# Graph attention on one core: the last pair of edge blocks in three pieces, and matmuls with one-hot matrices in place of a closing scatter

## What is computed

```python
h   = relu(layernorm(x)) @ W_node.T                 # per node, 4 heads x 32
att = leaky(sum([h[src], h[dst], edge @ W_edge.T] * a))   # per edge and head, slope 0.2
m   = max(segment_max(att, dst), 0)
ex  = exp(att - m[dst])
den = segment_sum(ex, dst) + (E - deg) * exp(-m)
out = x + segment_sum(ex / den[dst] * h[src], dst)
```

## Time and profile before

| | us |
|---|---|
| median of 3 runs | 4960.86 |
| the 3 runs | 4958.59, 4969.13, 4960.86 |
| profiled execution, its own time | 4962.95 |
| its span, first to last instruction | 4955.9 |
| DVE busy | 2412.0 (49%) |
| ACT busy | 1368.3 (28%) |
| PE busy | 777.3 (16%) |
| POOL busy | 3712.2 (75%) |

### The profile page before, as it was taken

The page is one execution under the profiler, slowest core; times in us unless marked ns, Lnnn a source line. Parts: engine busy times, 40 slices in busy tenths (PEclk is TensorE's granted clock), DMA queues, the critical chain, the costliest instruction groups (busy, mean ns, idle before and its releaser), DMA issues.

```text
span 4955.9 us, 14358 instructions
## 1 busy us (share of the span) xinstructions
PE 777.3 (16%) x1453; PEld 390.6 (8%) x1453; DVE 2412.0 (49%) x2384; ACT 1368.3 (28%) x1021; POOL 3712.2 (75%) x3530
## 2 busy tenths in 40 slices
PE   5321111111111111111111111111111111111100
PEld 3310000000000000000000000000000000000000
DVE  7337454545445454454544545445454454544543
ACT  7013232222322222222222322223222232222320
POOL 6667777777777777777777777777777777777766
PEclk9555555555555555555555555555555555555555
DMA  7234444343443434434344343433434434343353
GB/s 250 90 132 119 140 123 128 114 137 114 126 125 114 137 114 128 123 115 137 114 127 123 114 136 114 129 121 115 137 114 128 122 115 136 114 131 120 116 170 104
DMA packets 171831, 627.97 MB, mean 127 GB/s; under 512 B 72897, under 2 KB 73666, under 8 KB 155426
## 3 DMA queue, kind: packets, MB, share of 16 engines
q0 software_dynamic: 115936, 252.37, 21.0%
q1 hardware_dynamic: 55874, 375.39, 20.1%
HBM read 382.66 MB, written 244.86 MB: 127 GB/s over the span
## 4 chain that ended last, share of the span: by engine, by line
POOL 70%; issue 24%; another core or an unknown queue 2%; ACT 2%; DVE 1%; PE 0%; DMA 0%; POOLq 0%; ACTq 0%; DVEq 0%; SPq 0%
POOL slots L308 69%; ACT pen L375 1%; DVE pen L482 0%; PE ae L792 0%; DVE slots L496 0%; ACT big L392 0%; ACT slots L391 0%; POOL tdst_scratch L311 0%; ACT R L421 0%; PE wexp L785 0%; DMA state_scratch<-R 0%; DVE V L636 0%; DVE slots L501 0%; DMA cols<-in_cols_dram 0%
## 5 line engine op out<-in xcount | busy, mean ns | idle before, releaser
L308 POOL DMA_INDIRECT slots<-rows_scratch,idx x3224 | 3421.5, 1061 | 1066.5 <-issue 1066.5
L803 PE MATMUL ae<-eab,w_att 128*128 128x416 f32 x992 | 650.6, 829 | 3796.2 <-DMA eab<-in_ea_dram 2539.1
L603 DVE TENSOR_TENSOR z<-slots,big 128x104 f32<-128x104 f32 (+1 forms) x125 | 43.1, 345 | 2116.3 <-DMA slots<-rows_scratch,idx 1887.3
L636 DVE TENSOR_TENSOR_SCAN V<-A,V 128x1848 f32<-128x1848 f32 x248 | 993.7, 4007 | 35.4 <-issue 4.8
L421 ACT COPY R<-V 128x1716 f32<-128x1716 f32 x248 | 777.8, 3136 | 339.1 <-DVE V L636 196.7
L417 ACT ACTIVATE A<-D 128x1848 f32<-128x1848 f32 x246 | 419.7, 1706 | 744.7 <-DVE V L636 410.3
L803 PEld LDWEIGHTS ae<-eab,w_att 128*128 128x128 f32 x992 | 296.0, 313 | 4150.4 <-issue 3384.4
L626 DVE TENSOR_TENSOR V<-slots,wexp 128x1716 f32<-128x1716 f32 x125 | 404.8, 3239 | 22.4 <-issue 21.0
L626 DVE TENSOR_TENSOR V<-slots,extra 128x1716 f32<-128x1716 f32 x123 | 398.2, 3237 | 22.0 <-issue 16.3
L438 ACT ACTIVATE wexp<-D 128x104 f32<-128x104 f32 x62 | 16.2, 261 | 1092.5 <-DVEq L621 628.8
L438 ACT ACTIVATE extra<-D 128x104 f32<-128x104 f32 x61 | 15.9, 261 | 1063.2 <-DVEq L621 631.2
(11 more groups left out here) (168 smaller groups left out, 602.3 us busy)
## 6 DMA issues: line engine op xcount, KB each, us to landing
state_scratch<-R SPq DMA_DIRECT2D x123, 1768.0 KB
eab<-in_ea_dram SPq DMA_DIRECT2D x126, 832.0 KB
slots<-rows_scratch,idx POOLq DMA_INDIRECT x3224
rows_scratch<-slots SPq DMA_DIRECT2D x14, 476.0 KB
tdst_scratch<-eab SPq DMA_DIRECT2D x4, 1612.0 KB
big<-tdst_scratch SPq DMA_DIRECT2D x8, 806.0 KB
big<-in_x_t_dram SPq DMA_DIRECT2D x14, 448.0 KB, 4.3
big<-in_x_dram SPq DMA_DIRECT2D x7, 896.0 KB
```

Of the source, the lines that this page charges most:

```text
L308: pool.indirect_dma_start(buf, None, table, bass.IndirectOffsetOnAxis(ap=index, axis=0)).then_inc(done, 16)
L636: nc.vector.tensor_tensor_scan(V[:, v, :], a_all, V[:, v, :], 0.0, ALU.mult, ALU.add).then_inc(scanned, 1)
L803: last = mm(ps_ae[k][:, 0:KB * Q], w_att[:, a * P:(a + 1) * P], eab[:, k, a * KB * Q:(a + 1) * KB * Q], start=a == 0, stop=a == 3)
```

## The change

The last pair is worked on in three pieces of 13, 9 and 4 columns, with three waits, copies and stores in place of two. The buffers of the end (`pen_end`, `att_end`, `D2_end`, `M`) get a place per piece, and the tail's work area moves from V[:, 0] to V[:, 1].

The scatter at the end goes, with `x_first`, its gather, `fix_i` and the spare rows of the output. In its place the fix chain computes for each partition the difference between the merged result and the one that the ordinary path gives (`att_fix`), by three more vector instructions. For each group of 7, DVE compares a row of node numbers with the place of the node to be fixed (`one_hot`, 128 x 896), PE multiplies the seven one-hot matrices with `att_fix` (seven 128 x 128 matmuls into `ps_ae`), and DVE adds the product to `xr` in two instructions (`add_fix`), ahead of the group's ordinary work. `one_hot(0)`, `one_hot(1)` and `add_fix(0)` stand ahead of the group loop; in the loop, one_hot(g + 2) and add_fix(g + 1) follow the addition of group g. The wait for x_again moves from L757 into `add_fix`.

```diff
+LAST = ((0, KB), (KB, 9), (KB + 9, KB - 9))
...
-                    for v in range(2):
-                        dve.wait_ge(gather_end[v], 16 * KB)
-                        logits(p, k, 1 - v, v, KB, att_end, att_end, pen_end[:, v:v + 1, :, :], D2_end[:, v, :])
-                        dve.wait_ge(w_ready, p + 1 + v)
-                        if v == 0:
-                            dve.wait_ge(copied, p)
-                        sums(k, v, hk(w_exp[1 - v][:, 0:H * KB]), 2 * p + 1 + v, False)
+                    for e, (o, n) in enumerate(LAST):
+                        u = (p + e) % 2
+                        c = LAST[e + 1][1] + 1 if e + 1 < len(LAST) else COL
+                        dve.wait_ge(gather_end[e], 16 * n)
+                        logits(p, k, u, M_END[e], o, n, att_end[:, e, :], hk(att_end[:, e + 1, 0:H * c]), pen_end[:, e, 0:H * (n + 1)], D2_end[:, e, 0:H * (n + 1)])
+                        dve.wait_ge(w_ready, p + 1 + e)
+                        if e != 1:
+                            dve.wait_ge(copied, p + e // 2)
+                        m = LAST[e - 1][1] if e else KB
+                        sums(k, o, n, e % 2, hk(w_exp[u][:, 0:H * n]), 2 * p + 1 + e, vcols(1 - e % 2, m + 1)[:, :, m:m + 1])
...
-            pool.wait_ge(fix_ready, 1)
-            pool.wait_ge(stored, 16 * STEPS)
-            scatter(out[:, :], fix_i[:, 0:1], x_first[:, :], fix_dma)
...
+            nc.vector.tensor_scalar(fx[:, 3 * H:4 * H], s_first[:, VAL:ROW], -1.0, None, ALU.mult)
...
-            nc.vector.tensor_tensor(hv(x_first[:, :]), hv(x_first[:, :]), hv(cf[:, 0:VAL])[:, :, 0:HD], ALU.add).then_inc(fix_ready, 1)
-
+            nc.vector.tensor_tensor(hv(f["tmp"])[:, :, 0:HD], hv(s_first[:, 0:VAL])[:, :, 0:HD], wide(f["den"][:, H:2 * H], HD), ALU.mult)
+            nc.vector.tensor_tensor(hv(cf[:, 0:VAL])[:, :, 0:HD], hv(cf[:, 0:VAL])[:, :, 0:HD], wide(f["den"][:, 0:H], HD), ALU.mult)
+            dve.drain()
+            nc.vector.tensor_tensor(hv(att_fix[:, :]), hv(cf[:, 0:VAL])[:, :, 0:HD], hv(f["tmp"])[:, :, 0:HD], ALU.subtract).then_inc(fix_ready, 1)
+
+            def one_hot(g):
+                after(dve, moved, g - 1)
+                nc.vector.tensor_tensor(hot[g % 2], firsts[:, :].rearrange("p (a j) -> p a j", a=1).broadcast_to([P, NG, P]),
+                                        fix_at[:, g * NG:(g + 1) * NG].rearrange("p (w a) -> p w a", a=1).broadcast_to([P, NG, P]),
+                                        ALU.is_equal).then_inc(hot_done, 1)
+
+            def add_fix(g):
+                if g % 2 == 0:
+                    dve.wait_ge(x_again[g // 2], 16)
+                dve.wait_ge(moved, g + 1)
+                for k, (a, b) in enumerate(((0, 4), (4, NG))):
+                    xg = xr[:, g * NG + a:g * NG + b, :]
+                    last = nc.vector.tensor_tensor(xg, xg, ps_ae[k][:, 0:(b - a) * P].rearrange("p (w d) -> p w d", d=D), ALU.add)
+                last.then_inc(moved_taken, 1)
+
+            one_hot(0)
+            one_hot(1)
+            add_fix(0)
...
-                if g % 2 == 0:
-                    dve.wait_ge(x_again[g // 2], 16)
                 dve.drain()
                 xg = xr[:, g * NG:(g + 1) * NG, :]
                 nc.vector.tensor_tensor(xg, xg, A[:, g % 2 * 1024:g % 2 * 1024 + NG * D].rearrange("p (w d) -> p w d", d=D), ALU.add).then_inc(group_done, 1)
+                if g + 2 < STEPS:
+                    one_hot(g + 2)
+                if g + 1 < STEPS:
+                    add_fix(g + 1)
...
+            pe.wait_ge(fix_ready, 1)
+            for g in range(STEPS):
+                pe.wait_ge(hot_done, g + 1)
+                after(pe, moved_taken, g)
+                for n in range(NG):
+                    last = mm(ps_ae[n // 4][:, n % 4 * P:(n % 4 + 1) * P], hot[g % 2][:, n, :], att_fix[:, :], start=True, stop=True)
+                last.then_inc(moved, 1)
```

## The result

| | before | after |
|---|---|---|
| median of the runs, us | 4967.6 (4958.6 to 4969.1) | 5008.0 (4997.8 to 5011.4) |
| ratio | 1 | 1.0077, 95% interval 1.0066 to 1.0087 |
| profiled execution: own time / span, us | 4962.95 / 4955.9 | 5011.35 / 5009.5 |
| time around the span, us | 7.05 | 1.85 |

The change makes the kernel 0.8% slower, 40 us by the medians. The two profiled executions lie 48.4 us apart (5011.35 - 4962.95), where I had forecast 29.0. The direction and the place were right, but two steps of the sum were far off and their errors had opposite signs.

The account below looks back on a forecast made before the run. POOL's gathers bound the kernel now, VectorE's paced groups after the change. Group 0 at 4848.5, 13 x 9.7, last group 7.1, then 2.9: end 4984.9 against 4955.9, +29.0; forecast 4990 us, bounds 4945 to 5008.

Parts of the forecast that it names:

- The paced state: Closing stage: VectorE gets through one instruction, drains counted, per 0.78 us; main case, slower, spanning 4970 to 5008, chance 0.66.
- the rivals without a pace: Closing stage: VectorE needs 5.5 us per group and POOL bounds, -15.8, 4945 us, chance 0.18; POOL stretched builds on that.
- The price of an instruction: VectorE's group loop: 7.00 us over nine instructions, drains counted, gives 0.78 us for each.
- The head: Last pair in three pieces: last scan ends 2.0 us earlier, s_first starts at 4807.9, last gather ends 6.2 us earlier.
- The fix chain's three instructions: Three vector instructions added between the last scan and group 0, at 0.78 us each: 2.3 us.
- Between the fix chain and group 0: one_hot(0) 1.10, seven matmuls 3.0, two additions 1.1, hand-overs 0.3: 5.5 us, so group 0 starts at 4848.5.
- The groups: Closing group loop: 12.5 instructions instead of 9, period 9.7 us instead of 7.00, 13 periods, then 7.1 for the last group.
- POOL stretched: Closing stage: VectorE's new instructions slow 98 gathers by 0.15 us each, 14.7 on the no-pace end: 4960, chance 0.06.
- The end: Behind L760: closing scatter and its wait go, POOL's drain hidden, tail shrinks from 13.0 to 2.9 us, -10.1.
- Around the span: Execution's own time outside the span: 7.05 us, carried over from the kernel before.
- The signs I gave: Trace after: L747 over 9 us apart, idle at drains, last gather about 50 us before last L760, s_first near 4808.

Follow-up runs that it names:

- plus_three: Kernel before with three one-element memsets on VectorE behind each group's closing addition: 4995.0 us, ratio 1.0051.
- after_drains: Kernel after with eleven further drains on VectorE behind the last scan: 5009.4 us against 4972.5 for before on the same chip, ratio 1.0076.
- before_again: Kernel before, unchanged, run once more for its trace: 4958.3 us, one run.
- one_hot_only: Kernel after with the last pair in two pieces as before, one-hot matmuls kept: 5007.4 us, ratio 1.0050 to before.
- one_matmul: Kernel after with one of the seven matmuls in groups 1 to 13, VectorE's instructions unchanged: 4999.9 us, ratio 1.0061 to before.
- no_scatter: Kernel before without its closing scatter and the wait for it, leaving nodes that span partitions uncorrected: 4973.9 us, ratio 0.9995.
- free_matmuls: Kernel before with 98 matmuls on TensorE behind the fix chain, whose result nobody reads or waits for: 4985.1 us, ratio 1.0035.
- three_pieces: Kernel after with the x_first path and closing scatter of the kernel before, without the one-hot matmuls: 4990.7 us, ratio 1.0023 to before.

## Why the prediction was right or wrong

**The direction: right, and by the cause named.** The paced state decides, and the rivals without a pace did not come. The range held the median only at its very edge (5008.0 against a bound of 5008), and the forecast of 4990 was as near as it was only because errors cancelled, as shown below. The delay is idle time marked "issue" at drains, as read from the earlier trace rows, and short again where VectorE has had a long pause.

**The price of an instruction: wrong.** I divided 7.00 us by nine instructions, drains counted. The right count is five arithmetic instructions at 1.40 us each and drains at nothing (plus_three, after_drains). The earlier trace rows held a hint: POOL's main-loop gather takes 1.40 us, and I had noted that stretch without comparing it with the groups. Inside a group neighbours lie 0.7 to 2.5 us apart, so that only whole periods show the price, and a period of a single length cannot tell nine at 0.78 from five at 1.40; it took a second length.

**The head: wrong in sign.** The nine-column piece came as worked out: product 2.28 (2.24 forecast), scan 2.91 (2.86), and from the end of the small copy to s_first 3.0 us (3.4). But the four-column piece's scan ended at 32.9 us behind the mark and not at 28.0, held by idle times of 3.66, 1.42 and 1.17 us; s_first came 1.6 us earlier than before instead of 6.2. Before_again and one_hot_only differ by 1.3 us in that place, so even the 1.6 are hardly a gain. I had written that the pace could eat the head start. What I missed is that it does not stop there: the eleven instructions are a debt that the next drain collects, and the fix chain behind it ended 15.4 us later. I had moved it 2.0 us earlier.

**The fix chain's three instructions:** 2.3 forecast, 4.2 measured, by the price again.

**Between the fix chain and group 0:** 5.5 forecast, 16.9 measured (4869.28 to 4886.20). The matmuls took 3.2 us as forecast (3.0) and the additions 1.07, but between them VectorE was released 11.4 us late. Taken together, group 0 began 36.6 us later and not 5.8: the largest error of the sum, 30.8 us.

**The groups:** 126.4 us forecast from the first L787 to the last (13 x 9.7 is 126.1, and my sum carried 0.3 too much), 117.2 measured (4886.20 to 5003.43): 9.2 too much, and 3.9 too much for the last group, which was unhindered at 3.2 us. Nowhere was the period 9.7: it is 11.20 where only VectorE's pace counts (one_matmul), 7 to 27 where a wait for TensorE comes first, and 5.19 behind the long wait of 17.8 us and from 4972 on, where VectorE has either rested long enough or the pace is over. "TensorE's later groups lie beside VectorE's work and cost nothing" was wrong: 12.4 us. Nor did the wait of POOL for group_done stay met: it stood 7.3 and 14.0 us for VectorE, and its last gather ended 184.5 us behind the mark, not at the forecast 156.0. That cost nothing, since VectorE set the end.

**POOL stretched:** this rival did not come. Without those two waits a gather of the closing stage takes (95.9 + 29.3) / 98 = 1.28 us in the kernel after, against 1.25 in the earlier trace rows, which is 2.6 us over all 98 and off the path that sets the end.

**The end:** -10.1 forecast, -10.1 measured (2.9 us behind L798). The explanation was half right: POOL's drain ends 9.3 us behind its last gather and is hidden, but with VectorE on time it would be the end (no_scatter).

**Around the span:** I carried 7.05 us over; it was 1.85. In the kernel before three instruction packets land behind the span's end, near 4962.7, where the execution's own time of 4962.95 ends; in the kernel after there are none. The DMA view of before, from 4956 to 4970:

```profile
DMA packets 3, 0.02 MB, mean 2 GB/s; under 512 B 0, under 2 KB 0, under 8 KB 0
## 3 DMA queue, kind: packets, MB, share of 16 engines
q14 instruction: 3, 0.02, 0.6%
```

Of the other kernels no_scatter has 9.4 us around its span and before_again 6.9, all the rest 1.8 to 2.6. It is not a matter of the code alone: the unchanged kernel has 7.3 to 7.4 us around its span (medians) on the chips with the pace and 1.8 on the one without it. So these 5.2 us are no gain to count on, and what sets them stays open.

The errors: +30.8 before group 0, -9.2 and -3.9 in the groups, -5.2 around: 12.5, which is 41.5 - 29.0. The forecast was nearly the size of the result because two wrong counts met, which is luck.

**Two arguments that do not carry.** I took the nearness of the timed runs to the profiled one as support for the pace being real. But every run on record, of every kernel, lists a span and a granted clock, and those come from the profiler's records, so no run was made without them. That the pace comes from writing these records, and would be absent without them, is a rival that no run here tests. If it holds, the loss measured here would be smaller or gone in a run without records. And I wrote that the eleven groups before the last have long drains; in the earlier trace rows it is the median that is long, and group 12, right before the last, is as fast as the last one (L747 at 4931.65, L749 at 4931.91).

**The signs I gave.** "L747 of successive groups over 9 us apart, idle at drains": in one_matmul, not in the kernel after, where the idle time moved to the wait for TensorE. ACT waits for VectorE, by groups of instructions on ACT (from 4860 on), as I said:

```profile
L469 ACT ACTIVATE R<-slots 128x28 f32<-128x28 f32 x12 | 2.7, 227 | 137.9 <-DVE big L798 111.6 <-issue 26.4
```

The last gather ended 39.8 us before the last addition (50 forecast), and the span 2.9 us behind it (3). s_first came at 37.0 behind the mark, the equivalent of 4812.5 and not 4808.

**On the rule that a drain lasts the instruction's duration less 266 ns** (the Trainium skill, VectorE: DVE Perf Modes, The DRAIN you can't avoid): it would give nothing behind an L747 of 0.19 us. The chip without the pace comes near it, with 204 ns in all fourteen groups. On the chips with it the drain shows 3.05 us, but after_drains says that the time is not the drain's; the drain is only where the debt of the instructions ahead of it is collected.

**What stays open.** What makes the pace, whether it is there without the profiler's records, and why the runs on one chip lack it. Why VectorE was released 10 to 22 us after TensorE's last matmul in four groups: TensorE's own pace (28 loads and passes per group x 1.40 = 39 us) is more than any wait, and three groups follow the wait of 17.8 us without any, so that it does not fit as it stands; one_matmul shows only that the waits go when the matmuls are few and done before VectorE asks, and that a first one (13.8 us in the kernel after, with seven matmuls there too) stays. And whether the change pays on the chip without the pace: by the prediction's sum without one it would be 15.8 us faster, which is an estimate and was not measured.

I ran no version meant to beat the kernel before. The group loop of before ends 5.2 us behind its last gather (4942.92 - 4937.75) on either kind of chip, so fewer instructions on VectorE gain little there; what is left is the closing scatter, and no_scatter, which drops it without anything in its place, cannot be told from the kernel before (0.9995, interval 0.9986 to 1.0005).

## What to carry to other kernels

When idle time marked "issue" shows at drains, count the arithmetic instructions of a stretch, divide, and test the price with a few one-element memsets in a place where nothing waits: an added instruction of 0.07 us may cost 1.4. If the price is there, cut small work into fewer instructions, not into smaller ones; a further piece, a comparison or a separate addition can cost more than the transfer or the closing step that it saves. And compare at least two chips before such a change is judged, and runs without the profiler's records if you can: the same kernel differed by 490 us between two chips.

## What the runs showed of the hardware that I had not expected

- A pace of 1.40 us per instruction, on each engine by itself: VectorE's arithmetic instructions (5 in 7.00 us, 8 in 11.20), TensorE's loads and passes (2 in 2.80), GpSimd's gathers (1.40 each in the main loop). Eleven added drains cost nothing. After a pause an engine runs freely for a while: 42 loads and 42 passes on TensorE. It is not there from the start (TensorE's 624 loads and passes in the first 180 us took 0.29 us each), and it was seen only with the profiler's records on.
- The runs on one chip do not have it: 4478 us against 4968, gathers at 1.255 us in the main loop, with the same granted TensorE clock of 0.56.
- The pace lasts after GpSimd's gathers are over: to 4971.7 in plus_three, whose last gather ended at 4952.4, and to 4965.2 on TensorE in free_matmuls, whose last gather ended at 4941.8.
- GpSimd's gathers are issued 1.25 us apart in the closing stage even with the pace; the closing drain then takes until 13.6 us behind the last of the 98 (no_scatter). 99 x (1.40 - 1.25) = 14.9 us would be the debt; that this is the cause is argued, not shown.
- The profiles with the pace start the same code up to 21 us apart (the mark lies at 4771.2 in before_again and at 4792.6 in three_pieces), so that only intervals behind a common mark tell a few us.
